# Order of the transposes, first-pass units and output products in the attention part of a fused post-norm block

## The chip, the cores and the metric

The program runs on one NeuronCore of a Trainium2 chip. The metric is device time in microseconds (us), the median of several executions. The engines named here are TensorE (PE in the profile; PEld is its weight load), VectorE (DVE), ScalarE (ACT), GpSimd (POOL) and SyncE (SP, which issues most DMAs). Each engine works through its own instruction list in order, and waits are on semaphores.

## The reference

One transformer block with post-norm. The input is x of shape (2, 1024, 512), seen as 2048 tokens of 512 features.

```python
def attn(x, Wqk_w, Wqk_b, Wv_w, Wv_b, Wo_w, Wo_b):        # H = 8 heads of E = 8 features, HEAD_DIM = 64
    qk = (x @ Wqk_w.T + Wqk_b).reshape(b, n, H, E, 2)
    q, k = qk[..., 0], qk[..., 1]                          # both (b, H, n, E)
    v = (x @ Wv_w.T + Wv_b).reshape(b, n, H, E)
    scores = einsum('bhqd,bhkd->bhqk', q, k)
    attn = softmax(scores) / HEAD_DIM ** 0.5
    out = einsum('bhsl,bhlv->bhsv', attn, v)
    return out.reshape(b, n, H * E) @ Wo_w.T + Wo_b

def ffn(x, ...):                                           # int4 weights with a scale per group of 128 inputs
    return (silu(x @ Wg.T) * (x @ Wu.T)) @ Wd.T            # 512 -> 1792 -> 512

x = layernorm(x + attn(x))
x = layernorm(x + ffn(x))
```

## The kernel before

**Blocks and steps.** The 2048 tokens are four blocks of TB = 512 queries (NB = 4, numbered u = 0 to 3; two per batch entry). Attention goes through ALL = 64 steps n: for each block two groups g of HG = 4 heads (a pair u, g is numbered f = 0 to 7), and for each group KT = 8 tiles of 128 keys. So a group is 8 steps long, and the step number inside it is n % 8. A step has two halves, called pair 0 and pair 1. In each half PE makes the scores of two heads (`scores`, L1135: two matmuls on the two halves of the array's rows), ACT turns them into exponentials with one instruction of 1024 columns (`exps`, L817), and PE sums exponentials times V of the step before (`av`, L1164, into bank 6).

**First pass.** The maxima that the exponent needs come from an earlier pass over the scores. A unit of it is one matmul of 512 columns on one half of the array's rows (`first_pass`, L1057) and one DVE reduction (`reduce`, L1364). There are FIRST = 256 units, 32 for each f; they go through a ring of three PSUM banks (4, 5, 7), so PE may write unit m only when unit m-3 is reduced. The units run AHEAD = 46 in front, then four per step, two in each half. After every 32nd DVE combines them (`combine`, L1374); POOL splits the maxima in parts, PE turns them (`turn_maxima`, L1063) and SP puts them into the score operands. The last unit falls in step 52.

**Turns.** When a group is summed, ACT copies bank 6 to SBUF (`av_out`, tile avt, L824). PE turns this tile with four transposes of 128x128 (kind "avT", L1095) at the end of step 8f+10, which is the third step of the next group; ACT copies the result (`copy_sums`, L857) and POOL normalises it (`normalise`, L667 to L677). After both groups of a block the normalised sums are turned once more ("attT", L1103, two transposes, copied by L849) and multiplied by the output weights in two products of two token tiles each ("wo", k = 0 and 1, L1111), which ACT copies to the tile wob (L845) and POOL adds to x1 (`add_attention`, L651). For block 0 this happens inside the attention loop: attT in step 22, the products in steps 23 and 27 (`WO_AT = (7, 11)` after step 16). All of these share banks 0 to 3 with the scores, in the order of the list `shared`; each use waits until the use before the previous one is read.

**The drain.** From step DRAIN = 53 on there is no first pass and its banks are free. `ASIDE` names what goes there, one turn or product in the middle of a step, between the scores of pair 0 and pair 1: attT and wo of block 1, avT of f = 6, attT and wo of block 2. DVE reads these itself: `att_out` (L1447) copies attT, `add_output` (L1454) adds a product's tile to x1, `normalise` (L1383, L1386) normalises f = 6. In the drain the sums are made by `av_whole` (L1147, 512 columns). DVE's list there is written by hand: `attention_stats(0)` (L1394, four tiles of block 0), `mean_variance`, `att_out(1)`, `down_ratios`, two `add_output(1)`, `apply(0)` (L1412, block 0's normalised rows), `scale_ratios` (L1418 to L1427), two more `add_output(1)`, `normalise(6)`, `att_out(2)`, four `add_output(2)`. POOL splits the rows that `apply(0)` gives into two fp16 parts, and SP turns them with a DMA transpose (`turn_x1`, L498).

**Behind it.** After step 63 PE starts the feed-forward part with `gate(0, 0)` (L1175), which waits for the turned rows of block 0, for the gate and up weights and for all reads of the drain's products. The feed-forward part fills the rest of the program; its matmuls are L1175, L1187 and L1266. Block 3's turns and products lie in its first periods.

Of the kernel before, what the change touches and what calls it, by code (L numbers as in the profile page):

```python
# [21 lines left out]
P = 128  # L22
# [8 lines left out]
NB = T // TB  # L31
BT = TB // P
KT = N // P
# [7 lines left out]
STEPS = NG * KT  # L41
# [16 lines left out]
def build(nc, x, xT, wqkT, bqk, wvT, bv, woT, bo, gq, gs, uq, us, dq, ds, ds_next, spread, out):  # L58
    ctx = ExitStack()
    with ctx:  # L60
# [59 lines left out]
        ident = sb("ident", [P, P], F32)  # L120
# [159 lines left out]
        def turns_at(n, pair):  # L280

            if pair == 0:
                return []
            f, r = divmod(n + 3, KT)
            if r == 0 and f < NB * NG:
                return [("M", f, 0)]
            f, r = divmod(n - 10, KT)
            if r == 0 and 0 <= f < LASTF:
                return [("avT", f, 0)]
            r = n - STEPS  # L290
            if r == 6:
                return [("attT", 0, 0)]
            if r in WO_AT:
                return [("wo", 0, WO_AT.index(r))]
            return []

        WO_AT = (7, 11)
        LASTF = NB * NG - 2
        DRAIN = ALL - 11
        ASIDE = {DRAIN: ("attT", 1, 0), DRAIN + 1: ("wo", 1, 0), DRAIN + 3: ("wo", 1, 1), DRAIN + 4: ("avT", LASTF, 0),  # L300
                 DRAIN + 6: ("attT", 2, 0), DRAIN + 7: ("wo", 2, 0), DRAIN + 9: ("wo", 2, 1)}
        aside = list(ASIDE.values())
        copied = [use for use in aside for _ in range({"avT": 0, "attT": 1, "wo": 2}[use[0]])]
        copy_count = {use: i + 1 for i, use in enumerate(copied)}
# [38 lines left out]
        def shared_banks(*use):  # L343
            return 2 * ((shared_index[use] + 1) % 2)
# [191 lines left out]
        def _(pool):  # L536
# [142 lines left out]

            for f in range(2, NB * NG):  # L680
                normalise(f - 2)
                if f == 4:
                    for t in range(2, BT):
                        add_attention(0, t)
                split_max(f)
                if f == 2:
                    add_bias(0)
                if f in (2, 3, 4):
                    load_weights(f)
                if f == 4:  # L690
                    add_bias(1)
                if f in (5, 6):
                    add_bias(f - 3)
                if f == 3:
                    for t in range(2):
                        add_attention(0, t)
            inverse(0)
            for t in range(BT):
                x1_parts(0, t)
# [62 lines left out]
        def _(act):  # L762
# [76 lines left out]

            def wo_out(u, k):  # L840
                act.wait_ge(s_of, turn_count["wo", u, k])
                if u:
                    act.wait_ge(s_add, 2 * k + 2)
                at = shared_banks("wo", u, k)
                nc.scalar.activation(wob[:, 2 * k:2 * k + 2, :], ps[:, at:at + 2, :], ACT.Copy).then_inc(s_read, 1)  # L845

# [132 lines left out]
        def _(pe):  # L979
# [97 lines left out]
            def turn(kind, u, k):  # L1077
# [34 lines left out]
                                              start=True, stop=True)  # L1112
                mm.then_inc(s_of, 1)

            def scores(n, pair):

                u, s = divmod(n, STEPS)
                g, kt = divmod(s, KT)
                b, k = divmod(u, N // TB)
                pi = 2 * n + pair  # L1120
                if kt == 0 and pair == 0:
                    pe.wait_ge(s_mld[g], 16 * 2 * (u + 1))
                at = shared_banks("scores", n, pair)
                if pi >= 2:
                    wait_shared_read(pe, *shared[shared_index["scores", n, pair] - 2])
                elif pi == 0:

                    pe.wait_ge(s_vc, 2 * B)
                    pe.wait_ge(s_kept, len(placed) - 1)
                    pe.wait_ge(s_kept1, 1)  # L1130
                else:
                    pe.wait_ge(s_projr, 6)
                for j in range(2):
                    rows, t = slice(ROWS * j, ROWS * (j + 1)), 2 * g + pair
                    mm = nc.tensor.matmul(bank[at + j], ks[b][rows, t, kt * P:(kt + 1) * P],  # L1135
                                          qs[b][rows, k, t, :], start=True, stop=True)
                mm.then_inc(s_scf, 1)
# [53 lines left out]
            def piece(p):  # L1191
                p[0](*p[1:])
# [19 lines left out]
            for n, use in enumerate(before):  # L1212
                ring_use(*use)
                for p in later.get(n, []):
                    piece(p)
            for n in range(DRAIN):
                after_group_start = n % KT == 1
                for pair in range(2):
                    firsts_ahead = n and pair == 0 and turns_at(n - 1, 1)
                    if firsts_ahead:  # L1220
                        for use in ring_uses_at(n, pair):
                            ring_use(*use)
                    scores(n, pair)
                    if after_group_start and pair:
                        av(n - 1, 0)
                    if not firsts_ahead:
                        for use in ring_uses_at(n, pair):
                            ring_use(*use)
                    for use in turns_at(n, pair):
                        turn(*use)  # L1230
                    if n and (pair or not after_group_start):
                        av(n - 1, pair)
# [58 lines left out]
        def _(dve):  # L1291
# [95 lines left out]
                                        ALU.mult).then_inc(s_normd, 1)  # L1387

            def attention_stats(u, t):
                if 0 < u < NB - 1:  # L1390
                    dve.wait_ge(s_aside, copy_count["wo", u, t // 2] - 1 + t % 2)
                else:
                    dve.wait_ge(s_add, (BT if u else 0) + t + 1)
                nc.vector.bn_stats(st[:, t, :], x1[:, u * BT + t, :]).then_inc(s_bn, 1)  # L1394

            def mean_variance(n):
# [99 lines left out]
                  .then_inc(s_us[t % 2], 1)  # L1496

            for k in range(BT):
                attention_stats(0, k)
            mean_variance(0)  # L1500
            att_out(1)
# [21 lines left out]
            def down_out(t, k):  # L1523

                blk, i = divmod(t, G)
                if t == TILES - 1:
                    return
                dve.wait_ge(s_df[k], t + 1)
                if k == 0 and t in (0, LOW):
                    dve.wait_ge(s_rows[t // LOW], 16)  # L1530
                if t == LAST_BLOCK + k:
                    dve.wait_ge(s_resid, residual_count(k, k))
                    nc.vector.tensor_tensor(bank[k], bank[k], x1[:, BT * (NB - 1) + k, :], ALU.add).then_inc(s_dr[k], 1)
                    dve.wait_ge(s_dr[k], scaled_count(t - 1, k) + 1)
                dst, by = bank[k], down_row(i)
                if i == G - 1:
                    dst = wob[:, k, :]
                    if blk == 0:
                        dve.wait_ge(s_add, 2 * BT)
                    else:  # L1540
                        dve.wait_ge(s_tr, BT * (blk - 1) + k + 1)
                if t == TILES - 2:
                    dve.wait_ge(s_lastw, 1)
                    by = last_row
                nc.vector.tensor_tensor(dst, bank[k], by, ALU.mult).then_inc(s_dr[k], 1)  # L1545
# [98 lines left out]
```

## Time and profile before

| | |
|---|---|
| median of 3 runs | 515.64 us (515.24 to 515.70) |
| profiled execution | 515.92 us, of which the profile's span is 514.1 us |
| granted TensorE clock | 0.996 of full speed |
| PE busy | 499.8 us (97% of the span) |
| DVE busy | 409.0 us (80%) |
| ACT busy | 406.4 us (79%) |
| POOL busy | 282.9 us (55%) |
| first-pass reductions on DVE | 20.5 to 185.1 us |
| drain (scores of step 53 to `gate(0, 0)`) | 185.18 to 210.19 us |

How to read it: the busy share of PE is high everywhere, because matmuls are pipelined and short waits between them are covered by the end of the one before. What an engine waits for is therefore read from the start times in the timeline. A row of the timeline merges instructions of one kind that follow each other: it gives the start, the time to the end of the last, the engine, the line, the tiles, how many they are, and in brackets the idle time of the engine ahead of it with what ended it. Start times of successive rows on PE give what each piece costs there.

### The profile page before, as it was taken

To read this page: it belongs to the slowest core of one execution; us is meant where nothing else is said; L and a number is where in the kernel's file an instruction comes from. 1 tells how busy PE (TensorE), PEld (TensorE's weight loads), DVE (VectorE), ACT (ScalarE), POOL (GpSimd) and SP (SyncE) were. 2 spreads that over 40 slices of the span, in tenths; PEclk is the share of its full clock that TensorE was granted. 3 is DMA by queue.
4 is the path that set the end of the run, shared out by engine and by line. 5 is a ranking of instruction groups with operands and counts; after the bars stand their busy time and mean duration, and the time that the engine had idled before them with its cause. 6 is when DMAs were issued, how large, how long until landed. Compare 5 with 4: busy or idle time off the path is not lost.

```text
span 514.1 us, 8164 instructions
## 1 busy us (share of the span) xinstructions
PE 499.8 (97%) x2986; PEld 194.4 (38%) x2986; DVE 409.0 (80%) x688; ACT 406.4 (79%) x569; POOL 282.9 (55%) x330
## 2 busy tenths in 40 slices
PE   8999999999999999999999999999999999999994
PEld 3222233323333322334444444444444444444441
DVE  1799999999999996478778778778668666788676
ACT  1523898988989989867888888888888888888883
POOL 9200094845574355072664686676885874748741
PEclk9999999999999999999999999999999999999998
DMA  6420018953630007600031121130020020000022
GB/s 194 133 73 9 18 46 209 265 113 73 97 55 2 2 5 143 246 1 0 3 61 21 22 41 22 21 62 1 1 82 1 1 83 0 2 0 1 0 82 83
DMA packets 30153, 29.22 MB, mean 57 GB/s; under 512 B 19489, under 2 KB 21921, under 8 KB 29857
## 3 DMA queue, kind: packets, MB, share of 16 engines
q1 hardware_dynamic: 26544, 22.41, 15.6%
q0 software_dynamic: 3424, 6.03, 6.4%
q8 instruction: 24, 0.39, 0.3%
q10 hardware_dynamic: 144, 0.26, 0.1%
q14 instruction: 17, 0.13, 0.1%
HBM read 24.37 MB, written 4.23 MB: 56 GB/s over the span
## 4 chain that ended last, share of the span: by engine, by line
PE 89%; DVE 5%; ACT 3%; issue 1%; DMA 1%; SPq 0%; POOLq 0%; POOL 0%; DVEq 0%
PE ps L1187 19%; PE ps L1175 19%; PE ps L1266 18%; PE ps L1164 10%; PE ps L1057 8%; PE ps L1135 6%; PE ps L987 3%; ACT pbuf L817 3%; DVE mxh L1364 2%; PE ps L1111 1%; PE ps L1147 1%; DMA arena<-xT 1%; PE ps L1039 1%; PE ps L997 1%; PE ps L1095 1%
## 5 line engine op out<-in xcount | busy, mean ns | idle before, releaser
L1364 DVE TENSOR_REDUCE mxh<-ps 128x1 f32<-128x512 f32 x256 | 157.4, 682 | 4.7 <-PE ps L1057 3.7
L817 ACT ACTIVATE pbuf<-ps,gamma 128x1024 f32<-128x1024 f32 x128 | 137.1, 1114 | 15.5 <-PE ps L1135 12.7
L910 ACT ACTIVATE ps<-ps,ratio 128x512 f32<-128x512 f32 x167 | 105.8, 659 | 41.5 <-PE ps L1175 38.6
L1266 PE MATMUL ps<-wd,stack 128*128 128x512 f16 x440 | 129.6, 379 | 0.0
L1187 PE MATMUL ps<-arena,wu 128*128 128x512 f16 x448 | 115.4, 379 | 0.0
L1175 PE MATMUL ps<-arena,wg 128*128 128x512 f16 x448 | 115.4, 379 | 0.1
L1545 DVE TENSOR_TENSOR ps<-ps,stack 128x512 f32<-128x512 f32 x128 | 87.8, 695 | 32.3 <-PE ps L1266 30.3
L916 ACT ACTIVATE ps<-ps,ratio 128x512 f32<-128x512 f32 x156 | 98.9, 659 | 5.6 <-PE ps L1187 1.2
L712 POOL CAST stack<-pbuf 128x512 f16<-128x512 f32 x55 | 33.5, 609 | 74.4 <-DVE pbuf L1520 74.4
L1545 DVE TENSOR_TENSOR ps<-ps,pbuf 128x512 f32<-128x512 f32 x76 | 52.6, 695 | 23.2 <-PE ps L1266 22.6
L1164 PE MATMUL ps<-pbuf,arena 128*32 128x256 f32 x832 | 66.5, 391 | 0.5 <-ACT avt L824 0.2
L714 POOL TENSOR_TENSOR stack<-pbuf,stack 128x512 f16<-128x512 f32 x55 | 63.7, 1157 | 4.5
L1175 PEld LDWEIGHTS ps<-arena,wg 128*128 128x128 f16 x448 | 43.5, 98 | 54.4 <-issue 1.7
L1187 PEld LDWEIGHTS ps<-arena,wu 128*128 128x128 f16 x448 | 43.4, 98 | 54.2 <-DVE pbuf L1520 2.7
L1266 PEld LDWEIGHTS ps<-wd,stack 128*128 128x128 f16 x440 | 43.0, 98 | 52.1 <-DVE ps L1545 0.4
L1057 PE MATMUL ps<-stack 64*128 64x512 f16 x256 | 60.8, 382 | 1.3 <-DVE mxh L1364 0.6
L1135 PE MATMUL ps<-stack 64*128 64x512 f16 x256 | 50.4, 384 | 0.8 <-ACT pbuf L817 0.5
L1520 DVE SCALAR_TENSOR_TENSOR pbuf<-ps,scales,pbuf 128x512 f32<-128x512 f32 x56 | 41.9, 748 | 6.2 <-PE ps L1187 6.1
L924 ACT ACTIVATE pbuf<-ps,scales 128x512 f32<-128x512 f32 x56 | 38.0, 679 | 0.2 <-PE ps L1175 0.2
L1057 PEld LDWEIGHTS ps<-stack 64*128 64x128 f16 x256 | 20.9, 93 | 40.6 <-DVE mxh L1364 34.4
L667 POOL TENSOR_TENSOR inv<-av_s,minus 128x16 f32<-128x16 f32 x6 | 17.6, 2926 | 29.9 <-ACT av_s L857 29.9
L1135 PEld LDWEIGHTS ps<-stack 64*128 64x128 f16 x256 | 12.3, 92 | 48.0 <-issue 32.1
(133 smaller groups left out, 397.3 us busy)
## 6 DMA issues: line engine op xcount, KB each, us to landing
arena<-xT SPq DMA_DIRECT2D x16, 256.0 KB, 6.2
x<-x SPq DMA_DIRECT2D x2, 2048.0 KB, 9.8
out<-x SPq DMA_DIRECT2D x3, 1024.0 KB, 4.2
stack<-down_ratios SPq DMA_DIRECT2D x1, 2048.0 KB, 10.5
wg<-gq POOLq DMA_DIRECT2D x4, 448.0 KB, 7.4
wu<-uq POOLq DMA_DIRECT2D x4, 448.0 KB, 7.3
wd<-dq POOLq DMA_DIRECT2D x2, 896.0 KB, 10.9
pbuf<-down_ratios SPq DMA_DIRECT2D x1, 1536.0 KB, 6.4
```

What stands on the lines that cost most here:

```text
L714: nc.gpsimd.tensor_tensor(mparts[:, 1, t % NM, :], sg[t % 2], mparts[:, 0, t % NM, :], ALU.subtract)\
L817: nc.scalar.activation(pbuf[:, pi % 4, :].rearrange("p (a n) -> p a n", a=2), ps[:, at:at + 2, :], ACT.Exp, scale=gamma[:, n // (ALL // B) ...
L910: nc.scalar.activation(gbank[t % 2], gbank[t % 2], ACT.Copy, scale=gr[:, t % G, c:c + 1])\
L916: nc.scalar.activation(ubank[t % 2], ubank[t % 2], ACT.Copy, scale=ur[:, t % G, c:c + 1])\
L1057: nc.tensor.matmul(ring_bank("first", n), qs[b][rows, k, t, qt * P:(qt + 1) * P], ks[b][rows, t, half * TB:(half + 1) * TB], start=True, s ...
L1135: mm = nc.tensor.matmul(bank[at + j], ks[b][rows, t, kt * P:(kt + 1) * P], qs[b][rows, k, t, :], start=True, stop=True)
L1164: mm = nc.tensor.matmul(bank[AVB][j * VC:(j + 1) * VC, lo:hi], vst[b][:, kt, g * HG + j, :], pbuf[:, (2 * n + j // 2) % 4, (j % 2) * TB + ...
L1175: mm = nc.tensor.matmul(gbank[t % 2], wg[:, c, i * P:(i + 1) * P], x1v[blk][:, a, c, :, :], start=(c == 0 and a == 0), stop=(a == 1), skip ...
L1187: mm = nc.tensor.matmul(ubank[t % 2], wu[:, c, i * P:(i + 1) * P], x1v[blk][:, a, c, :, :], start=(c == 0 and a == 0), stop=(a == 1), skip ...
L1266: mm = nc.tensor.matmul(bank[k], mparts[:, a, t % NM, k * P:(k + 1) * P], wd[:, i, :], start=(i == 0 and a == 0), stop=(a == 1), skip_grou ...
L1364: nc.vector.tensor_reduce(mxh[:, f % 2, qh, half:half + 1], ring_bank("first", n), AX.X, ALU.max)\
L1545: nc.vector.tensor_tensor(dst, bank[k], by, ALU.mult).then_inc(s_dr[k], 1)
```

## The change

1. The turn of the sums avT of f = 0 to 5 (steps 10, 18, ..., 50) is cut into two halves of two transposes. A single first-pass unit stands behind each half, taken from the next half step. From there the units run half a step early: in the next step the pairs stand in front of the sums as usual but belong to the half step behind, and in the step after it the first half has none; there one pair stands between the two sums, and with it the order is the old one again.
2. Block 0's two products (wo, k = 0 and 1) leave steps 23 and 27 and go to the first two steps of the drain, 53 and 54. What was there moves: attT of block 1 from step 53 to 55, its products from 54 and 56 to 56 and 58, attT of block 2 from step 59 to 60, its products from 60 and 62 to 61 and 62. avT of f = 6 stays in step 57.
3. The products of block 0 are no longer copied by ACT and added by POOL. DVE adds them (`add_output(0, k)`), and each addition stands ahead of the statistics of its tile. Two waits that guarded wob fall away, and `down_out` waits for four additions of POOL in place of eight.

```diff
-            r = n - STEPS
-            if r == 6:
+            if n == STEPS + 6:
                 return [("attT", 0, 0)]
-            if r in WO_AT:
-                return [("wo", 0, WO_AT.index(r))]
...
-        WO_AT = (7, 11)
         LASTF = NB * NG - 2
         DRAIN = ALL - 11
-        ASIDE = {DRAIN: ("attT", 1, 0), DRAIN + 1: ("wo", 1, 0), DRAIN + 3: ("wo", 1, 1), DRAIN + 4: ("avT", LASTF, 0),
-                 DRAIN + 6: ("attT", 2, 0), DRAIN + 7: ("wo", 2, 0), DRAIN + 9: ("wo", 2, 1)}
+        ASIDE = {DRAIN: ("wo", 0, 0), DRAIN + 1: ("wo", 0, 1), DRAIN + 2: ("attT", 1, 0), DRAIN + 3: ("wo", 1, 0),
+                 DRAIN + 4: ("avT", LASTF, 0), DRAIN + 5: ("wo", 1, 1), DRAIN + 7: ("attT", 2, 0),
+                 DRAIN + 8: ("wo", 2, 0), DRAIN + 9: ("wo", 2, 1)}
...
-                if f == 4:
-                    for t in range(2, BT):
-                        add_attention(0, t)
...
-                if u:
-                    act.wait_ge(s_add, 2 * k + 2)
...
+            def half_turn(f, part):
+                if part == 0:
+                    wait_shared_read(pe, *shared[shared_index["avT", f, 0] - 2])
+                    pe.wait_ge(s_ave, f + 1)
+                dst = bank[shared_banks("avT", f, 0)]
+                for t in range(part * BT // 2, (part + 1) * BT // 2):
+                    mm = nc.tensor.transpose(dst[:, t * P:(t + 1) * P], avt[:, f % 2, t * P:(t + 1) * P], ident[:])
+                if part:
+                    mm.then_inc(s_of, 1)
...
             for n in range(DRAIN):
+                after_turn = n % KT - 2
+                if n >= KT + 2 and after_turn == 0:
+                    scores(n, 0)
+                    firsts(n, 0)
+                    av(n - 1, 0)
+                    scores(n, 1)
+                    firsts(n, 1)
+                    half_turn(n // KT - 1, 0)
+                    firsts(n + 1, 0, slice(0, 1))
+                    half_turn(n // KT - 1, 1)
+                    firsts(n + 1, 0, slice(1, 2))
+                    av(n - 1, 1)
+                    continue
+                if n >= KT + 2 and after_turn == 1:
+                    scores(n, 0)
+                    firsts(n, 1)
+                    av(n - 1, 0)
+                    scores(n, 1)
+                    firsts(n + 1, 0)
+                    av(n - 1, 1)
+                    continue
+                if n >= KT + 2 and after_turn == 2:
+                    scores(n, 0)
+                    av(n - 1, 0)
+                    firsts(n, 1)
+                    scores(n, 1)
+                    av(n - 1, 1)
+                    continue
...
             def attention_stats(u, t):
-                if 0 < u < NB - 1:
+                if u < NB - 1:
                     dve.wait_ge(s_aside, copy_count["wo", u, t // 2] - 1 + t % 2)
...
             for k in range(BT):
+                add_output(0, k)
                 attention_stats(0, k)
             mean_variance(0)
             att_out(1)
```

The order on PE at the first turn (step 10), before. L1057 is a first-pass unit, L1095 the turn, L1164 the sums, L1135 the scores.

```order
L1057 MATMUL ps<-stack0 128x512 x2
L1095 MATMUL ps<-ident,avt 128x128 x4
L1164 MATMUL ps<-pbuf,arena 32x256 x4
L1057 MATMUL ps<-stack0 128x512 x2
L1135 MATMUL ps<-stack0 128x512 x2
L1164 MATMUL ps<-pbuf,arena 32x256 x4
```

The same place now; a unit is L1046 and a half turn L1111 here.

```order
L1046 MATMUL ps<-stack0 128x512 x2
L1111 MATMUL ps<-ident,avt 128x128 x2
L1046 MATMUL ps<-stack0 128x512
L1111 MATMUL ps<-ident,avt 128x128 x2
L1046 MATMUL ps<-stack0 128x512
L1164 MATMUL ps<-pbuf,arena 32x256 x4
L1135 MATMUL ps<-stack0 128x512 x2
L1046 MATMUL ps<-stack0 128x512 x2
```

The next pair of units moved ahead of the sums, one unit behind each half of the turn. On PE from the second half of step 11 on, two half steps later, it now reads:

```order
L1046 MATMUL ps<-stack0 128x512 x2
L1164 MATMUL ps<-pbuf,arena 32x256 x4
L1135 MATMUL ps<-stack0 128x512 x2
L1164 MATMUL ps<-pbuf,arena 32x256 x4
L1046 MATMUL ps<-stack0 128x512 x2
L1135 MATMUL ps<-stack0 128x512 x2
```

Between the two pairs of units there now stand two sums with one pair of scores between them; ahead of the change one sum and one pair of scores stood between any two pairs. The order on DVE behind the last reduction, before (BN_STATS are the statistics, BN_AGGR mean and variance, COPY `att_out(1)`, the five on stack0 `down_ratios`):

```order
L1394 BN_STATS st<-x1 128x6 x4
L1404 BN_AGGR mv<-st 128x2 x4
L1447 COPY attT<-ps 128x256
L1433 TENSOR_TENSOR stack0<-stack0 128x120
L1435 TENSOR_SCALAR stack0<-stack0 128x120
L1438 TENSOR_TENSOR stack0<-stack0 128x120
L1440 RECIPROCAL stack0<-stack0 128x60
L1442 TENSOR_TENSOR stack0<-stack0 128x60
L1454 TENSOR_TENSOR x1<-ps,x1 128x512 x2
L1412 TENSOR_SCALAR x1<-x1,mv,rstd 128x512 x4
```

The same place on DVE now:

```order
L1489 TENSOR_TENSOR x1<-ps,x1 128x512
L1429 BN_STATS st<-x1 128x6
L1489 TENSOR_TENSOR x1<-ps,x1 128x512
L1429 BN_STATS st<-x1 128x6
L1489 TENSOR_TENSOR x1<-ps,x1 128x512
L1429 BN_STATS st<-x1 128x6
L1489 TENSOR_TENSOR x1<-ps,x1 128x512
L1429 BN_STATS st<-x1 128x6
L1439 BN_AGGR mv<-st 128x2 x4
L1482 COPY attT<-ps 128x256
```

Four additions stand ahead of the statistics, one each; all that follows on DVE, down to the copy of attT of block 2, keeps its order.

## Rows read from the trace of the kernel before

**Rows 1.** Busy time by stretch: three spans of eight steps, then the drain.

```profile
core 0: us, PE busy (x) PEld busy (x) DVE busy (x) ACT busy (x) POOL busy (x), PEclk, DMA share, GB/s
79.22:99.07 19.85, 19.78 (x199) 6.23 (x197) 19.61 (x33) 17.98 (x19) 11.59 (x15) 1.00 0.91 253
99.07:120.57 21.50, 21.11 (x205) 6.51 (x203) 20.06 (x33) 19.17 (x21) 9.56 (x16) 1.00 0.76 147
120.57:141.59 21.02, 20.76 (x203) 6.30 (x201) 19.95 (x33) 18.89 (x20) 13.79 (x15) 1.00 0.41 62
...
185.20:210.20 25.00, 23.05 (x162) 6.11 (x159) 16.93 (x35) 23.40 (x25) 9.56 (x15) 1.00 0.54 140
```

**Rows 2.** Timeline of DVE: reductions behind a turn and behind a product.

```profile
79.25 3.81 DVE L1364 TENSOR_REDUCE mxh<-ps 128x1 f32<-128x512 f32 x6 [0.17 <-PE ps L1057]
...
83.18 15.76 DVE L1364 TENSOR_REDUCE mxh<-ps 128x1 f32<-128x512 f32 x26
...
112.78 3.81 DVE L1364 TENSOR_REDUCE mxh<-ps 128x1 f32<-128x512 f32 x6 [0.83 <-PE ps L1057]
```

**Rows 3.** Timeline of PE: first turn, block 0's attT, last turn.

```profile
77.26 0.47 PE L1057 MATMUL ps<-stack 64*128 64x512 f16 x2
77.66 0.66 PE L1095 MATMUL ps<-ident,avt 128*128 128x128 f32 x4
78.25 0.64 PE L1164 MATMUL ps<-pbuf,arena 128*32 128x256 f32 x8
78.82 0.39 PE L1057 MATMUL ps<-stack 64*128 64x512 f16 x2
79.05 0.38 PE L1135 MATMUL ps<-stack 64*128 64x512 f16 x2
...
107.97 0.44 PE L1103 MATMUL ps<-ident,att 128*128 128x128 f32 x2
108.34 0.64 PE L1164 MATMUL ps<-pbuf,arena 128*32 128x256 f32 x8
...
179.74 0.66 PE L1095 MATMUL ps<-ident,avt 128*128 128x128 f32 x4
```

**Rows 4.** Timeline of ACT: the exponentials behind the first turn.

```profile
79.47 5.48 ACT L817 ACTIVATE pbuf<-ps,gamma 128x1024 f32<-128x1024 f32 x5 [0.71 <-PE ps L1135]
```

**Rows 5.** The page's group of the exponentials: count, busy, mean ns, idle before.

```profile
L817 ACT ACTIVATE pbuf<-ps,gamma 128x1024 f32<-128x1024 f32 x128 | 137.1, 1114 | 15.5 <-PE ps L1135 12.7
```

**Rows 6.** Timeline of PE in the drain: its start, a product step, its end.

```profile
185.18 0.39 PE L1135 MATMUL ps<-stack 64*128 64x512 f16 x2
...
204.25 0.69 PE L1135 MATMUL ps<-stack 64*128 64x512 f16 x4
...
205.88 0.39 PE L1135 MATMUL ps<-stack 64*128 64x512 f16 x2
206.10 1.02 PE L1111 MATMUL ps<-wo_s,attT 64*128 64x512 f32 x4
206.96 0.38 PE L1135 MATMUL ps<-stack 64*128 64x512 f16 x2
207.27 1.07 PE L1147 MATMUL ps<-pbuf,arena 128*32 128x512 f32 x8
...
210.19 0.60 PE L1175 MATMUL ps<-arena,wg 128*128 128x512 f16 x2
```

**Rows 7.** Timeline of DVE in the drain.

```profile
185.26 2.46 DVE L1394 BATCH_NORM_STATS2 st<-x 128x6 f32<-128x512 f32 x4
...
191.15 3.04 DVE L1412 TENSOR_SCALAR x<-x,mv,rstd 128x512 f32<-128x512 f32 x4
...
199.18 0.29 DVE L1386 TENSOR_TENSOR att<-ps,rec 128x128 f32<-128x128 f32 x1
...
207.24 1.29 DVE L1454 TENSOR_TENSOR x<-ps,x 128x512 f32<-128x512 f32 x2 [2.73 <-PE ps L1111]
```

**Rows 8.** Timeline of SP: the DMA transposes of block 0's rows.

```profile
194.39 6.37 SPq L498 DMA_TRANSPOSE arena<-split  x4
```

**Rows 9.** The page's DMA issues: KB each, median us to landing.

```profile
arena<-split SPq DMA_TRANSPOSE x16, 3.1
```

More of the change, by code:

```diff
@@ L693, in _ @@
                     add_bias(f - 3)
-                if f == 3:
-                    for t in range(2):
-                        add_attention(0, t)
             inverse(0)
@@ L1215, in _, with firsts @@
                     piece(p)
+            def firsts(n, pair, which=slice(None)):
+                for use in ring_uses_at(n, pair)[which]:
+                    ring_use(*use)
             for n in range(DRAIN):
+                after_turn = n % KT - 2
[26 more added lines that the diff above has]
+                    continue
                 after_group_start = n % KT == 1
@@ L1389, in attention_stats @@
             def attention_stats(u, t):
-                if 0 < u < NB - 1:
+                if u < NB - 1:
                     dve.wait_ge(s_aside, copy_count["wo", u, t // 2] - 1 + t % 2)
                 else:
-                    dve.wait_ge(s_add, (BT if u else 0) + t + 1)
+                    dve.wait_ge(s_add, t + 1)
                 nc.vector.bn_stats(st[:, t, :], x1[:, u * BT + t, :]).then_inc(s_bn, 1)
@@ L1538, in down_out @@
                     if blk == 0:
-                        dve.wait_ge(s_add, 2 * BT)
+                        dve.wait_ge(s_add, BT)
                     else:
```

## The prediction

> **What bounds the kernel now.** I read three views: the busy times by stretch, then the timelines of DVE and PE around one turn, then both in the drain. The change touches attention alone (up to 210 us). Behind it PE runs the feed-forward part with 97% busy over the whole page, so what attention's end gains or loses goes to the program's end one for one.
>
> In the attention loop DVE is the bound. Eight steps take 19.85 us, with DVE busy for 19.61 [rows 1]; 26 reductions take 15.76 us in a row [rows 2], so one follows the other every (15.76 - 0.68) / 25 = 0.60 us (0.68 is one whole reduction). A half step needs two, 1.21 us. From the PE rows one half step costs 0.57 (the sums until the next, 78.25 to 78.82) + 0.22 or 0.23 (scores or a pair of units) + 0.31 (a pair on half the rows until work on all rows, 206.96 to 207.27) = 1.11 us [rows 3, 6]. So PE has some 0.1 us to spare per half step, and the ring lets it bank two units at most. A turn costs PE 0.59 us (77.66 to 78.25), five half steps' worth of slack; so DVE runs dry once behind each turn (0.17 us shown ahead of 79.25) and for 0.83 us behind the first product [rows 2].
>
> In the drain no unit runs. PE is busy for 23.05 and ACT for 23.40 of 25.00 us [rows 1]; they alternate in holding each other. DVE has a long list there, without a gap from 185.26 to 199.18 + 0.29 = 199.47 [rows 7]. `attT` of block 2 on PE waits for the end of just this list (`normalise(6)`).
>
> **Part 1: the products leave steps 23 and 27.** Block 0's eight steps take 21.50 and the next eight 21.02 us against 19.85 [rows 1]: 1.65 + 1.17 = 2.82 us more. `attT` stays in step 22: it costs PE 0.37 us (107.97 to 108.34) [rows 3], of which I leave 0.34 as a loss: that is the more than usual distance of the reductions between `attT` and the first product's gap. Gain: 2.82 - 0.34 = **2.48 us**. ACT loses two copies of 1.02 us that only mattered there.
>
> **Part 2: the cut turns.** I walk the first turn in the new order with the costs above. A half turn costs 0.37 (as `attT`'s two transposes), so two halves cost 0.74 in place of 0.59. A single unit between transposes I price like a pair ahead of work on all rows, 0.31, since both members of a pair run at once: two singles cost 0.62, the pair ahead of scores 0.23 (78.82 to 79.05) [rows 3]. Both bounds of this price: nothing but its 0.22 above, and 0.40 if the return to transposes costs once more.
>
> The walk, from the same state: half turn 77.66, unit 78.03, half turn 78.34, unit 78.71, sums 79.02, scores 79.59, pair 79.82, sums 80.13, scores 80.70, pair 80.92 (its second member waits for its bank, 80.98), sums 81.30, scores 81.87. The next sums could start at 82.19, but they need both exponentials of the step before. The scores of 80.70 give theirs 0.42 later (79.05 to 79.47 [rows 3, 4]), it takes 1.11 us [rows 5], and some 0.06 pass until PE sees it: 82.29. The pair behind them starts at 82.86 and reaches DVE 0.43 later (78.82 to 79.25 [rows 2, 3]), at **83.29**. DVE started this very unit at 83.18 before [rows 2]. So the gap of 79.25 is gone, but DVE runs dry ahead of 83.29 for about 0.4 us instead: it has used up the units made early, and one half step brought none.
>
> PE is now also later. Next pair: 82.86 + 0.23 (scores) + 0.32 (sums) + 0.57 (scores) + 0.22 = 84.20, at DVE 84.63 against 83.18 + 2 x 0.60 = 84.38. The following sums wait for their exponential (83.09 + 0.42 + 1.11 + 0.06 = 84.68), so the pair behind is at 84.68 + 0.57 + 0.22 = 85.47, at DVE 85.90 against 85.58: **0.32 us late**. From there DVE is the bound again, in both orders. Five turns cost 5 x 0.32 = 1.60 us. At the sixth no unit is left behind it and PE alone counts: from the half turn to the scores of step 53 the walk takes 82.29 + 0.57 + 0.32 + 0.57 - 77.66 = 6.09 us, against 185.18 - 179.74 = 5.44 [rows 3, 6]: 0.65. Loss: **2.25 us**. Its bounds: with singles at their bare 0.22, no cost for cutting the turn and no wait for the exponential the same walk brings DVE 0.24 us earlier per turn (6 x 0.24 = 1.4 us gain); with 0.40 each it brings it 0.2 later still (3.5 us loss). I stay with 2.25, since each price has a row of its own kind.
>
> On the single units the Trainium skill ("TensorE: Matmul & The Clock Gate", Part 3: Packing small matmuls) says that matmuls on different row groups run at once, and that only a weight load for row groups not in use is pulled ahead. By it a lone 64-row unit next to 128-row transposes overlaps with nothing, which speaks against this order; the trace's pair costs 0.23 and 0.31 for two.
>
> **Part 3: the drain.** S is the start of step 53. A product costs PE 0.86 us (206.10 to 206.96), a plain step 1.63 (204.25 to 205.88), of which its sums 1.00; a product step is 0.22 + 0.86 + 0.31 + 1.00 = 2.39 [rows 6]. The two added products cost PE 1.72 us, and a good part of it falls into time that PE waited (25.00 - 23.05 = 1.95 us [rows 1]). Walking PE alone I get `attT` of block 2 (step 60) at about S + 17.65: seven steps of 1.63, four products, two turns, and 2 us of waits for exponentials and for banks.
>
> But DVE's list is longer and starts later. The first addition needs its product: S + 0.22, plus 1.14 until DVE has it (206.10 to 207.24 [rows 6, 7]) = S + 1.36. Each addition takes 0.68 and its statistics must wait for it: 0.74 + 0.60 = 1.34 per tile. Two tiles: S + 4.04. The second product needs both banks read: S + 3.50, so DVE has it at S + 4.64, and its two tiles' statistics end at S + 4.64 + 2 x 1.34 + 0.08 = S + 7.40. From the end of the statistics (185.26 + 2.46 = 187.72) to the end of `normalise(6)` (199.47) DVE needs 11.75 us without a gap [rows 7]: **S + 19.15**, where before it was 199.47 - 185.18 = S + 14.29. PE starts `attT` 0.15 later, S + 19.30, having waited 1.65 us. Queued behind it on PE are the second scores and the sums of step 60, so ACT stands too. From there: 0.37 + 0.32 + 1.00 = 1.69, step 61 with its product 2.39, step 62 2.39 + 0.15 (its banks are read 1.14 + 1.29 + 0.1 after the product before), step 63 1.63: `gate(0, 0)` at S + 27.55 against 25.01 before. Loss: **2.54 us**. Bounds: 0.9 if the list of DVE is in time (PE alone), 3.2 if additions and statistics cost 0.16 more per tile.
>
> What is hidden anyway: `apply(0)` moves from S + 5.97 to about S + 10.8. The last transpose was issued by 194.39 + 6.37 = 200.76 and lands 3.1 later [rows 8, 9], S + 18.7; 4.9 later is S + 23.6, ahead of the gate's S + 27.55 by 4 us. If the cover of DVE's wait goes, it is still ahead. The waits dropped at wob cost and give nothing: POOL and ACT come to them long after.
>
> **Sum.** -2.48 + 2.25 + 2.54 = +2.3 us. Against the profiled execution 515.92 that is 518.2; the median of the runs lies 0.28 lower. Forecast **518.0 us**.
>
> **The rivals.** (a) *The turns are neutral*: single units and split turn cost PE nothing net, because the gap they fill pays for them. -2.48 + 0 + 2.54 = +0.1: 515.7 us. For it: the 0.17 us gap is real and is filled. Against: the half step without units comes before PE has regained time.
> (b) *The turns gain, and the kernel is faster.* It decides at the pair behind the two sums of step 12: if it reaches DVE by 82.8 us on the old clock, no gap opens; the bare-cost bound gives that. -2.48 - 1.4 + 2.54 = -1.3: 514.3 us; with 0.39 us of each turn won (the reductions between 78.40 and 82.37 against 0.60 apiece) 513.3. Against: the wait for the exponential alone, 0.1 us, spends the margin.
> (c) *DVE's list is in time in the drain*: -2.48 + 2.25 + 0.9 = +0.7: 516.3 us. Against: the list has no gap today and gets four operations and a wait more.
> (d) *Both are dearer*: singles at 0.40 and additions with more delay: -2.48 + 3.5 + 3.2 = +4.2: 519.8 us.
> The Trainium skill ("Perfetto Trace Analysis", Identifying Dependency Chains) says to find the gaps of the bound engine and let what ends them start sooner. For one gap this change does that, which would speak for (b); no row shows the engine staying fed afterwards.
>
> **How the numbers follow.** Forecast 0.60; (a) 0.13; (b) 0.10; (c) 0.10; (d) 0.07. A measurement here tells some 0.2%, 1.0 us, from no change. Faster by that is (b), 0.10; the same is (a) and most of (c), 0.20; slower the rest, 0.70. The range reaches over (c) and half of (a) below and most of the way to (d): 515.4 to 519.4.
>
> **What would show it.** Right: no gap left at the products; a gap of 0.3 to 0.5 us on DVE just behind each combine, released by the first-pass matmul, in place of 0.17 behind the turn; eight steps at 20.1 to 20.2 us; `attT` of block 2 released by DVE's `att`, with over 1 us of idle PE ahead; the drain 27 to 28 us long. Wrong: eight steps at or under 19.85 (part 2), or a drain under 26.5 (part 3), or any change in length behind `gate(0, 0)`.

## The result and the profile after

The changed kernel takes 518.02 us (median of six runs, 517.71 to 518.25) against 515.45 us for the kernel before measured beside it (515.12 to 515.70). The ratio is 1.0049 with a 95% interval of 1.0039 to 1.0059: 2.6 us slower. The forecast was 518.0 with a range of 515.4 to 519.4. One of the twelve executions of the last experiment (e10) took 705.4 us at a granted clock of 0.656, and its time there is the median of the other eleven.

The profiled execution has a span of 516.1 us, only 2.0 above the 514.1 of before. The loop began 0.66 us earlier in it: the reductions behind the second combine start at 62.67 us, against 63.33 in the earlier trace, on stretches that the change doesn't touch. So I compare lengths inside each trace and not times since the start. First the busy times by stretch (as [rows 1]), for three stretches of eight steps, the drain and the rest:

```profile
core 0: us, PE busy (x) PEld busy (x) DVE busy (x) ACT busy (x) POOL busy (x), PEclk, DMA share, GB/s
82.65:102.86 20.21, 20.00 (x199) 6.28 (x197) 19.77 (x34) 18.20 (x20) 11.54 (x15) 1.00 0.95 268
102.86:123.43 20.57, 20.25 (x201) 6.39 (x199) 19.95 (x34) 18.36 (x21) 7.01 (x14) 1.00 0.58 112
123.43:143.63 20.20, 19.99 (x199) 6.28 (x197) 19.76 (x34) 18.19 (x20) 11.33 (x13) 1.00 0.59 92
184.49:212.19 27.70, 24.93 (x170) 6.76 (x166) 19.76 (x38) 23.91 (x25) 9.31 (x13) 1.00 0.42 106
212.19:516.10 303.91, 297.32 (x1370) 132.62 (x1366) 225.06 (x365) 247.49 (x393) 186.36 (x192) 1.00 0.11 32
```

The stretches that held 21.50 and 21.02 us [rows 1] now hold 20.57 and 20.20; those without a product went from 19.85 up to 20.2. From 63.33 to the scores of step 53 the loop took 185.18 - 63.33 = 121.85 us, now 184.49 - 62.67 = 121.82. The drain went from 25.01 to 27.70. The rest is 303.91 us in both traces (514.1 - 210.19 before). So all of the loss shows in the drain, and in the loop a gain and a loss cancel, as e1 shows below.

Where DVE runs dry in the loop (as [rows 2]): the timeline of its reductions and combines in the changed kernel.

```profile
62.67 19.40 DVE L1399 TENSOR_REDUCE mxh<-ps 128x1 f32<-128x512 f32 x32
82.11 0.18 DVE L1409 TENSOR_TENSOR mx<-mxh 128x16 f32<-128x16 f32 x1
82.65 19.63 DVE L1399 TENSOR_REDUCE mxh<-ps 128x1 f32<-128x512 f32 x32 [0.37 <-PE ps L1046]
```

The 0.17 us behind the turn and the 0.83 us behind each product are gone. A gap of 0.37 us behind each combine is new, five times. PE around the first turn (as [rows 3]):

```profile
77.00 0.44 PE L1111 MATMUL ps<-ident,avt 128*128 128x128 f32 x2
77.37 0.39 PE L1046 MATMUL ps<-stack 64*128 64x512 f16 x1
77.69 0.44 PE L1111 MATMUL ps<-ident,avt 128*128 128x128 f32 x2
78.06 0.39 PE L1046 MATMUL ps<-stack 64*128 64x512 f16 x1
78.38 0.64 PE L1164 MATMUL ps<-pbuf,arena 128*32 128x256 f32 x8
...
80.28 0.44 PE L1046 MATMUL ps<-stack 64*128 64x512 f16 x2
80.65 0.64 PE L1164 MATMUL ps<-pbuf,arena 128*32 128x256 f32 x8
81.22 0.39 PE L1135 MATMUL ps<-stack 64*128 64x512 f16 x2
81.65 0.64 PE L1164 MATMUL ps<-pbuf,arena 128*32 128x256 f32 x8
82.22 0.39 PE L1046 MATMUL ps<-stack 64*128 64x512 f16 x2
```

From the pair at 80.28 to the pair at 82.22 there are 1.94 us in which DVE can reduce 3.2 units and gets two; the two early ones are used up by then. The sums of 81.65 stand 0.43 behind the scores of 81.22, where 0.32 is the plain distance: the wait for the exponential. In the drain, PE's timeline at step 60 and the end of DVE's list (as [rows 6, 7]):

```profile
201.88 0.39 PE L1135 MATMUL ps<-stack 64*128 64x512 f16 x2
203.85 0.41 PE L1092 MATMUL ps<-ident,att 128*128 128x128 f32 x2 [1.58 <-issue]
```

```profile
189.25 0.69 DVE L1489 TENSOR_TENSOR x<-ps,x 128x512 f32<-128x512 f32 x1 [0.66 <-PE ps L1100]
...
198.38 0.67 DVE L1453 TENSOR_TENSOR small<-scales 128x112 f32<-128x112 f32 x1
...
203.46 0.29 DVE L1421 TENSOR_TENSOR att<-ps,rec 128x128 f32<-128x128 f32 x1
```

PE is idle for 1.58 us ahead of `attT` of block 2. The trace calls the reason "issue", but the matmul starts 0.10 us after DVE's `att` is done at 203.75, on which it waits. PE waits for DVE twice more, ahead of block 0's second product (step 54) and of block 1's first (step 56):

```profile
188.02 1.13 PE L1100 MATMUL ps<-wo_s,attT 64*128 64x512 f32 x4 [0.25 <-DVE x L1489]
...
192.86 1.13 PE L1100 MATMUL ps<-wo_s,attT 64*128 64x512 f32 x4 [0.17 <-DVE attT L1482]
```

They start 0.65 and 0.56 us behind the scores ahead of them, where 0.22 is the plain distance. The first waits until DVE's additions have read its banks, the second for DVE's copy of attT.

### The profile page after: what moved, and what is told of

The parts are those of the page before. It is cut to its first block, busy times and chain, and to the rows that moved or that the text cites. A ratio compares the mean times of both kernels' runs of the same rounds, so it can differ in the third digit from the quotient of the medians.

```text
span 516.1 us, 8162 instructions
## 1 busy us (share of the span) xinstructions
PE 501.5 (97%) x2986; PEld 195.3 (38%) x2986; DVE 411.9 (80%) x692; ACT 406.3 (79%) x567; POOL 277.7 (54%) x326
## 4 chain that ended last, share of the span: by engine, by line
PE 91%; DVE 4%; ACT 2%; issue 1%; DMA 1%; POOLq 0%; SPq 0%; POOL 0%; DVEq 0%
PE ps L1175 19%; PE ps L1187 19%; PE ps L1301 18%; PE ps L1164 11%; PE ps L1046 8%; PE ps L1135 6%; PE ps L976 3%; PE ps L1147 2%; PE ps L1100 2%; DVE mxh L1399 1%; ACT pbuf L808 1%; PE ps L1028 1%; PE ps L986 1%; DMA arena<-xT 1%; PE ps L1111 1%
## 5 line engine op out<-in xcount | busy, mean ns | idle before, releaser
L808 ACT ACTIVATE pbuf<-ps,gamma 128x1024 f32<-128x1024 f32 x128 | 138.6, 1113 | 17.3 <-PE ps L1135 14.2
L1164 PE MATMUL ps<-pbuf,arena 128*32 128x256 f32 x832 | 66.5, 391 | 1.2
L1046 PE MATMUL ps<-stack 64*128 64x512 f16 x256 | 61.0, 382 | 1.3 <-DVE mxh L1399 0.6
L1135 PE MATMUL ps<-stack 64*128 64x512 f16 x256 | 50.2, 385 | 0.3 <-ACT x L762 0.2
L1046 PEld LDWEIGHTS ps<-stack 64*128 64x128 f16 x256 | 21.3, 93 | 38.0 <-DVE mxh L1399 31.3
L1135 PEld LDWEIGHTS ps<-stack 64*128 64x128 f16 x256 | 12.4, 92 | 48.3 <-issue 39.5
```

The source lines that it names most:

```text
L808: nc.scalar.activation(pbuf[:, pi % 4, :].rearrange("p (a n) -> p a n", a=2), ps[:, at:at + 2, :], ACT.Exp, scale=gamma[:, n // (ALL // B) ...
L1046: nc.tensor.matmul(ring_bank("first", n), qs[b][rows, k, t, qt * P:(qt + 1) * P], ks[b][rows, t, half * TB:(half + 1) * TB], start=True, s ...
L1164: mm = nc.tensor.matmul(bank[AVB][j * VC:(j + 1) * VC, lo:hi], vst[b][:, kt, g * HG + j, :], pbuf[:, (2 * n + j // 2) % 4, (j % 2) * TB + ...
```

## The experiments

My theory has three terms: the products' leaving the loop gains 2.5 us, six turns cost 2.4, the drain costs 2.7, most of it because PE waits for DVE's list. The rivals say that the turns are neutral, or that PE or ACT set the drain's pace anyway.

**e1, old turns.** The three branches for the steps behind a turn are taken out, so the turn is again one piece in its old place.

```diff
             for n in range(DRAIN):
-                after_turn = n % KT - 2
-                if n >= KT + 2 and after_turn == 0:
...
-                    continue
                 after_group_start = n % KT == 1
```

> The changed kernel with the six turns of avT put back as they were; block 0's products stay in the drain. Theory (turns cost 2.4 us, products' leaving the loop gains 2.45, the drain costs 2.7): 518.0 - 2.4 = 515.6 us, that is within 0.3 us of the kernel before, with eight steps at 19.85 us, a drain of 27.7 us and DVE's 0.17 us gap back behind each turn. Rival (the turns are neutral and the drain and the loop's other steps cost it all): 518.0 us.

It took 515.85 us, ratio 1.0005 (0.9996 to 1.0014) to the kernel before. DVE's timeline and the first product of the drain:

```profile
82.77 15.75 DVE L1368 TENSOR_REDUCE mxh<-ps 128x1 f32<-128x512 f32 x26
98.69 3.81 DVE L1368 TENSOR_REDUCE mxh<-ps 128x1 f32<-128x512 f32 x6 [0.17 <-PE ps L1046]
102.62 16.12 DVE L1368 TENSOR_REDUCE mxh<-ps 128x1 f32<-128x512 f32 x26
```

```profile
182.54 1.02 PE L1100 MATMUL ps<-wo_s,attT 64*128 64x512 f32 x4
...
210.01 0.60 PE L1175 MATMUL ps<-arena,wg 128*128 128x512 f16 x2
```

Eight steps are back at 19.85 us (102.62 - 82.77) and the 0.17 us gap is back. The product stands 0.22 behind the scores of step 53, so these start at 182.32 and the drain is 27.69 us. From 62.91, where the reductions behind the second combine start, the loop is 119.41 us: 2.44 less than before, which is the gain of the products, and 2.41 less than with the new turns, which is their cost.

**e2, new turns alone.** The kernel before with the new order of turns and units; products and drain are left as they were. The product of step 27 stands where the other turns do:

```diff
                 if n >= KT + 2 and after_turn == 1:
                     scores(n, 0)
                     firsts(n, 1)
                     av(n - 1, 0)
                     scores(n, 1)
                     firsts(n + 1, 0)
+                    for use in turns_at(n, 1):
+                        turn(*use)
                     av(n - 1, 1)
                     continue
```

> The kernel before with the new turns alone (cut in two, single units between, units half a step early), products in steps 23 and 27 and drain as before. Theory: 515.45 + 2.4 = 517.8 us (0.5 less if the product of step 27 covers part of its turn), eight steps without a product at 20.2 us, drain 25.0 us. Rival (turns neutral): 515.5 us.

It took 517.65 us, ratio 1.0042 (1.0028 to 1.0055), near the forecast of 517.8: with the products and the drain's order as they were, the new turns make the kernel 2.2 us slower. The trace shows that this is a sum of two things. The reductions behind the second combine, the scores of step 53, the first product and the drain's end:

```profile
62.52 19.41 DVE L1412 TENSOR_REDUCE mxh<-ps 128x1 f32<-128x512 f32 x32
```

```profile
186.87 0.39 PE L1146 MATMUL ps<-stack 64*128 64x512 f16 x2
...
189.98 1.02 PE L1111 MATMUL ps<-wo_s,attT 64*128 64x512 f32 x4
...
211.46 0.60 PE L1186 MATMUL ps<-arena,wg 128*128 128x512 f16 x2
```

The loop takes 186.87 - 62.52 = 124.35 us, 2.50 more than before, but the drain 24.59 in place of 25.01. The last reductions end earlier with respect to step 53, so DVE comes sooner to the statistics and to the copy of attT, and the first product no longer waits for it: it starts 3.11 us behind the scores of step 53, before 188.59 - 185.18 = 3.41. The forecast had a drain of 25.0, so that the time still comes close to it is partly luck.

**e3, scale_ratios cut in three.** The changed kernel; of the five operations that lead to the scale ratios, one stays, one goes behind `normalise(6)`, three behind `att_out(2)`.

```diff
-            scale_ratios()
+            scale_ratios((0,))
             for t in range(2, BT):
                 add_output(1, t)
             normalise(LASTF)
+            scale_ratios((1,))
             att_out(2)
+            scale_ratios((2,))
```

> The changed kernel with scale_ratios on DVE cut in three: its first operation stays, the second goes behind normalise(6), the other three behind att_out(2). Theory (PE waits 1.6 us in step 60 for DVE's list and for nothing else there): 518.0 - 1.6 = 516.4 us, drain 26.0 us, attT of block 2 without idle PE time over 0.3 us ahead. Rival (another wait, for the second product's banks or the exponentials, takes its place): 517.5 us or more.

It took 516.90 us, ratio 1.0024 (1.0015 to 1.0034): 1.1 us less than the changed kernel, where I had expected 1.6. PE in and around step 60:

```profile
201.72 0.39 PE L1135 MATMUL ps<-stack 64*128 64x512 f16 x2
202.04 0.44 PE L1092 MATMUL ps<-ident,att 128*128 128x128 f32 x2
202.72 0.39 PE L1135 MATMUL ps<-stack 64*128 64x512 f16 x2 [0.24 <-ACT pbuf L808]
```

The wait for DVE is gone altogether; `attT` follows the scores by 0.32. But the scores behind it now wait 0.24 us for an exponential, which the stall had covered. The drain is 210.71 - 184.33 = 26.38 us, 1.32 shorter. That is a wait of the kind that the rival names, with a sixth of the stall's size. So the wait for the end of DVE's list accounts for 1.32 of the 2.69 us that the drain costs, about half; the other 1.37 stays in this run.

**e4, both.** e1 and e3 together.

> Old turns and scale_ratios cut in three, products of block 0 in the drain. Theory: the two effects add, 518.0 - 2.4 - 1.6 = 514.0 us, 1.4 us faster than the kernel before. Rival (PE or ACT takes up the drain's gain): 515.5 us.

It took 514.45 us, ratio 0.9981 (0.9973 to 0.9990), faster than the kernel before by 1.0 us. The two effects add: 2.2 and 1.1 from the single runs make 514.7. The forecast of 514.0 was too low mainly because it took the stall of 1.6 us as won in full.

**e5, turn in one piece, early pair.** The changed kernel with the whole turn first and the two early units behind it.

```diff
                     half_turn(n // KT - 1, 0)
-                    firsts(n + 1, 0, slice(0, 1))
                     half_turn(n // KT - 1, 1)
-                    firsts(n + 1, 0, slice(1, 2))
+                    firsts(n + 1, 0)
```

> The changed kernel with the turn in one piece and the two early units behind it as a pair, instead of two half turns with a single unit each; the half step without units stays. Theory (cutting costs 0.15 and single units 0.3 us of PE per turn, the rest of a turn's 0.35 to 0.4 us is the empty half step): eight steps at 20.0 us instead of 20.2, DVE still dry for 0.2 to 0.3 us behind the combine, 518.0 - 1.1 = 516.9 us. Rival (the cut is what costs and the early units are harmless): eight steps at 19.85 or less, 515.8 us. Rival (the empty half step is all): 518.0.

It took 517.39 us, ratio 1.0035 (1.0022 to 1.0047): between the rivals, but only half of the gain I had forecast. PE at the first turn, and DVE later on:

```profile
76.90 0.66 PE L1111 MATMUL ps<-ident,avt 128*128 128x128 f32 x4
77.49 0.68 PE L1046 MATMUL ps<-stack 64*128 64x512 f16 x2
78.10 0.64 PE L1164 MATMUL ps<-pbuf,arena 128*32 128x256 f32 x8
```

```profile
143.16 19.56 DVE L1398 TENSOR_REDUCE mxh<-ps 128x1 f32<-128x512 f32 x32 [0.34 <-PE ps L1046]
163.26 19.56 DVE L1398 TENSOR_REDUCE mxh<-ps 128x1 f32<-128x512 f32 x32 [0.34 <-PE ps L1046]
```

The pair takes 0.61 us instead of 0.31: its second unit waits for a bank of the ring. With cuts and singles the sums started 1.38 us behind the turn (77.00 to 78.38), here 1.20. So a good part of the saved PE time is spent on waiting for the ring, and eight steps take 20.10 us.

**e6, pair ahead of the sums.** The changed kernel, with the pair of the third step in front of its first sums, so that the half step without units comes one later.

```diff
                 if n >= KT + 2 and after_turn == 2:
                     scores(n, 0)
-                    av(n - 1, 0)
                     firsts(n, 1)
+                    av(n - 1, 0)
                     scores(n, 1)
```

> The changed kernel with one pair of units of step n%8 = 4 moved in front of the first sums of that step, so that the empty half step comes one half step later. Theory (what is missing is PE time behind the turn, not this pair's place): the 0.37 us gap behind the combine goes, a gap of about as much opens one pair later, eight steps at 20.1 us, 517.6 us (0.1 us less per turn). Rival (the late pair is the cause): eight steps at 19.7 to 19.85 us, 515.7 us or less.

It took 517.95 us, ratio 1.0048 (1.0032 to 1.0064), as the changed kernel. DVE:

```profile
143.06 0.18 DVE L1409 TENSOR_TENSOR mx<-mxh 128x16 f32<-128x16 f32 x1
143.15 1.28 DVE L1399 TENSOR_REDUCE mxh<-ps 128x1 f32<-128x512 f32 x2
144.90 18.30 DVE L1399 TENSOR_REDUCE mxh<-ps 128x1 f32<-128x512 f32 x30 [0.47 <-PE ps L1046]
```

The gap behind the combine is gone and one of 0.47 us stands two reductions later. In both places of the empty half step DVE runs dry behind it, and eight steps take 20.18 us (163.33 - 143.15) against 20.20: what is missing is PE time behind the turn, not this pair's place.

**e7, additions in pairs, on e4.** DVE adds two tiles of block 0 and then takes the statistics of both, so that PE's second product finds its banks read sooner and no statistics wait for the addition just ahead.

```diff
-            for k in range(BT):
-                add_output(0, k)
-                attention_stats(0, k)
+            for j in range(0, BT, 2):
+                for k in (j, j + 1):
+                    add_output(0, k)
+                for k in (j, j + 1):
+                    attention_stats(0, k)
```

> The kernel of e4 with DVE's additions of block 0 in pairs ahead of two statistics each, so that PE's second product finds its banks read 0.6 us sooner and no statistics wait for their own addition. Theory: PE's waits of 0.42 us in step 54 and 0.34 us in step 56 go, the drain is 25.7 us instead of 26.38, the time 514.45 - 0.6 = 513.8 us. Rival (ACT, with 23.4 us of work in the drain, takes it up): drain 26.2 us, 514.3 us.

It took 513.65 us, ratio 0.9966 (0.9954 to 0.9978): 1.9 us faster than the kernel before. The stretch of the drain:

```profile
182.00:207.61 25.61, 24.61 (x169) 6.69 (x165) 19.65 (x39) 23.60 (x25) 9.58 (x15) 1.00 0.39 94
```

25.61 us against 26.38 in e4. ACT still has 2 us to spare, so its rival falls. The products of steps 54 and 56 in this run:

```profile
185.11 1.02 PE L1100 MATMUL ps<-wo_s,attT 64*128 64x512 f32 x4
...
189.60 1.13 PE L1100 MATMUL ps<-wo_s,attT 64*128 64x512 f32 x4
```

They start 0.23 us (185.11 - 184.88) and 0.32 us (189.60 - 189.28) behind their scores, in place of 0.65 and 0.56: 0.66 of the 0.77 us by which the drain is shorter than in e4.

**e8, additions in pairs alone.** The same edit on the changed kernel, with new turns and scale_ratios whole.

> The changed kernel with only DVE's additions of block 0 in pairs, scale_ratios whole. Theory (the end of DVE's list sets the drain one for one): the list ends 0.65 us sooner, attT of block 2 as much sooner, drain 27.05 us, 517.4 us. Rival (PE's own pace sets it): no more than 0.2 us.

It took 517.16 us, ratio 1.0034 (1.0020 to 1.0047). PE:

```profile
201.05 0.39 PE L1135 MATMUL ps<-stack 64*128 64x512 f16 x2
203.04 0.41 PE L1092 MATMUL ps<-ident,att 128*128 128x128 f32 x2 [1.59 <-issue]
```

Both PE and DVE come earlier, by about the same: the scores of step 60 stand 16.62 us behind those of step 53 at 184.43 (before the edit 201.88 - 184.49 = 17.39), and PE still waits 1.59 us. `attT` moves from S + 19.36 to S + 18.61, the drain from 27.70 to 26.94 us. DVE's `att` is done at 202.93, 18.50 behind the scores of step 53, where it was 19.26. Since both moved alike, the length of the drain alone would not tell them apart; the wait of 1.59 us, with `attT` 0.11 behind DVE's `att`, does: what counts here is the end of DVE's list. A run in which PE alone comes sooner was not made.

**e9, attT of block 0 one step later.** On e7, in step 23 instead of 22.

> The kernel of e7 with block 0's attT one step later (step 23 instead of 22), two steps behind the turn of the maxima instead of one. Theory (a piece of PE work costs DVE only what PE has not yet regained from the piece before): the 0.34 us that attT costs in its eight steps shrink to 0 to 0.15, 513.65 - 0.25 = 513.4 us. Rival (each piece costs DVE its own length wherever it stands): 513.65 us, those eight steps stay at 20.2 us.

It took 513.63 us, ratio 0.9964 (0.9952 to 0.9976), the same as e7. The rival was right: the piece costs as much in either place. PE and DVE there:

```profile
109.32 0.44 PE L1092 MATMUL ps<-ident,att 128*128 128x128 f32 x2
...
113.66 0.64 PE L1164 MATMUL ps<-pbuf,arena 128*32 128x256 f32 x8 [0.19 <-ACT avt L815]
```

```profile
102.19 12.31 DVE L1368 TENSOR_REDUCE mxh<-ps 128x1 f32<-128x512 f32 x20
114.66 3.68 DVE L1368 TENSOR_REDUCE mxh<-ps 128x1 f32<-128x512 f32 x6 [0.16 <-PE ps L1046]
```

DVE loses time behind `attT` and once more at 114.66, where it runs dry for 0.16 us; together its eight steps take 20.24 us (122.43 - 102.19), in e7 20.22. Two steps on, the first sums of the next group wait for ACT's copy of the sums. That wait is not new, though: they start 0.58 us behind their scores here (113.08 to 113.66) and 0.55 in e7 (113.21 to 113.76), where DVE does not run dry behind them. Whether `attT` could be free elsewhere stays open.

**e10, the cut alone.** On e7: each turn cut in two, one half ahead of the sums and one behind, the units where they always were.

```diff
                     for use in turns_at(n, pair):
-                        turn(*use)
+                        if use[0] == "avT":
+                            half_turn(use[1], 0)
+                        else:
+                            turn(*use)
                     if n and (pair or not after_group_start):
                         av(n - 1, pair)
+                    for use in turns_at(n, pair):
+                        if use[0] == "avT":
+                            half_turn(use[1], 1)
```

> The kernel of e7 with each of the six turns cut in two halves, one ahead of the sums and one behind them, and the units where they always were. Theory (cutting costs PE 0.15 us, and DVE gets the next units as much later): DVE's gap behind a turn grows from 0.17 to 0.32 us, eight steps take 20.0 us, 513.65 + 0.9 = 514.55 us. Rival (the cut is free, and all that the new turns cost is the early units and the empty half step): 513.65 us.

It took 514.61 us, ratio 0.9984 (0.9975 to 0.9993), 0.96 more than e7. DVE:

```profile
142.65 15.76 DVE L1374 TENSOR_REDUCE mxh<-ps 128x1 f32<-128x512 f32 x26
158.72 3.81 DVE L1374 TENSOR_REDUCE mxh<-ps 128x1 f32<-128x512 f32 x6 [0.31 <-PE ps L1046]
162.65 15.76 DVE L1374 TENSOR_REDUCE mxh<-ps 128x1 f32<-128x512 f32 x26
```

The gap is 0.31 us and eight steps take 20.00. Two transposes on their own cost 0.37 us twice, four in a row 0.59, and in this order DVE pays that difference in full: 0.15 us, six times. It is nearly half of the 0.35 us that a new turn costs in eight steps. In e5, where the cut was taken away and the early pair stayed, eight steps got only 0.10 us shorter, because the pair behind the whole turn waits for its bank. So the parts do not simply add, and how the rest divides between the single units and the empty half step is not shown.

## Why the prediction was right

- **What bounds the loop.** It was DVE at 0.60 us per reduction, with PE close behind. Right: each run in which PE lost time behind a turn lengthened the eight steps, and the gaps shown here were released by the first-pass matmul.
- **Products out of the loop: -2.48 us.** e1 shows -2.44.
- **The new turns: +2.25 us.** Measured 2.41 (the changed kernel against e1 in their loops). The runs of e2 give 2.2, but that is 2.50 lost in its loop and 0.42 won in its drain. The walk of the first turn met the trace closely. It was made on a clock 0.66 us later; less that, it gave 77.37, 77.68, 78.05 and 78.36 for the pieces behind the first half turn, the trace has 77.37, 77.69, 78.06 and 78.38. The pair behind the empty half step came to 82.20 by the walk and stands at 82.22; DVE takes it at 82.65 against 82.63. Per turn I had 0.32 us, the trace has 0.35; at the last one 0.65, the trace 184.49 - 178.38 - 5.44 = 0.67. What made it hold was pricing each piece by a row with the same neighbour (a unit ahead of work on all rows at 0.31, not at its bare 0.22; two transposes at 0.37, not at half of 0.59), and following the exponential that the sums need.
- **The drain: +2.54 us.** Measured 27.70 - 25.01 = 2.69. DVE's list ended at 203.75 - 184.49 = S + 19.26 (S + 19.15 forecast), `attT` started at S + 19.36 (19.30), PE had waited 1.58 us (1.65). PE alone would have been there at S + 17.65; in e3, with the wait gone, it is there at 202.04 - 184.33 = S + 17.71. The small remainder is behind `attT`. Of the wait ahead of `attT`, 1.58 us long, e3 gave back 1.32.
- **Rivals.** (a) and (b), neutral or gaining turns, fall with e1 and e2; (d) falls with a single unit's 0.32 us against its 0.40 and with the drain's 2.69 against its 3.2. (c), a DVE list that is in time, falls with the trace and with e3 and e8. Its price was a little low, however: without the wait the drain costs 1.37 us more than before (e3), not 0.9. PE's way to `attT` was right to 0.06 us (S + 17.71 against 17.65); the rest is behind it. From `attT` to `gate(0, 0)` e3 takes 210.71 - 202.04 = 8.67 us, where I had 8.25: step 60's second scores wait for an exponential, so from `attT` to the next step it is 2.00 us in place of 1.69, and step 62 takes 2.69 in place of 2.54. The waits for DVE in steps 54 and 56 were part of the way to `attT`; e7 takes them away, `attT` comes at S + 16.94 (198.94 - 182.00), and the drain then costs 0.60.
- **What was luck.** The forecast is 0.02 us from the measured 518.02, but the shift was 2.57 us and I had 2.3. All three terms came out less favourable than forecast, by 0.04, 0.16 and 0.15 us, and the starting value was 0.19 above the median of the kernel before that was measured beside the changed one (515.64 against 515.45). The two errors hide each other.
- **Rule and trace.** By the Trainium skill ("TensorE: Matmul & The Clock Gate", Part 3: Packing small matmuls), as the prediction reads it, a lone unit next to full-height transposes overlaps with nothing. The trace agrees: the singles took 0.32 us each (77.37 to 77.69), as much as a pair ahead of work on all rows. The Trainium skill's advice to let what ends the gap start sooner ("Perfetto Trace Analysis"; it stands under Optimization Strategy, next to the section that the prediction names) did close the gap it was aimed at, and another opened behind it; in e6 the gap moved again.

## What to carry to other kernels

A piece of work on a nearly full engine that feeds a bound one through a short ring was paid by the bound engine here, wherever the gap showed; units fed early only moved the gap, and cutting the piece made it longer. Taking two products out of the loop altogether won 2.4 us there, but the drain lost 2.7 (e1: no change in sum), about half of it because the engine that took over their additions had an in-order list whose end another engine waits for. Leaving these additions with ACT and POOL in the drain was not tried. Before work is moved to such an engine, look at who waits for the last entry of its list, and move what is needed only later (here the scale ratios) behind it: products in the drain, old turns, scale ratios cut up and additions in pairs gave 513.65 us, 0.34% faster than the kernel before.

## What the runs showed of the hardware

- On DVE the statistics of a tile start 0.73 us behind the addition just ahead that makes it (185.86 to 186.59); two additions in a row are 0.60 apart. With two additions first (e8) the list ends 0.76 us sooner with the same operations. Of this, 0.42 is that the second product finds its banks read sooner (it starts 3.11 us behind the scores of step 53, not 3.53); from the first addition of the second pair to the end of its statistics the list is 2.48 us long instead of 2.74.
- A pair of units on the two halves of the rows cost 0.31 us in front of work on all rows, a single one 0.32. The second of a pair was nearly free only when its bank was: in e5, where it waits for a reduction, the pair took 0.61.
